# A 5120-row graph layer on one Trainium2 core: a third product summed in spare banks between rows of the second sweep

## The reference, cut to what matters

```
e   = blockwise (par * (diag * x) @ W + x)
h   = adj @ (adj.T @ e)
x1  = layernorm(x + layernorm(h) * gamma + beta + x)      # layer 0
T0  = x1
T1  = adj @ T0
T2  = 2 * adj @ T1 - T0
T3  = 2 * adj @ T2 - T1
out = layernorm(x1 + T0 @ w0 + T1 @ w1 + T2 @ w2 + T3 @ w3 + bias)   # layer 1
```

## Time and profile before

| what | value |
|---|---|
| median of 3 runs | 1223.32 us (1223.15 to 1223.8) |
| the profiled execution, its own time | 1222.88 us |
| its span in the profile | 1221.1 us |
| busy share of PE, DVE, ACT, POOL | 91%, 76%, 27%, 21% |
| moved over the span | 350.82 MB, mean 287 GB/s |
| second sweep | 866.0 to 1025.4 us |
| third sweep with its outputs | 1025.4 to 1206.7 us |

### The profile page before, as it was taken

The page is one execution under the profiler, slowest core; times in us unless marked ns, Lnnn a source line. Parts: engine busy times, 40 slices in busy tenths (PEclk is TensorE's granted clock), DMA queues, the critical chain, the costliest instruction groups (busy, mean ns, idle before and its releaser), DMA issues.

```text
span 1221.1 us, 13860 instructions
## 1 busy us (share of the span) xinstructions
PE 1109.2 (91%) x4995; PEld 480.7 (39%) x5004; DVE 928.5 (76%) x960; ACT 332.0 (27%) x594; POOL 257.0 (21%) x420
## 2 busy tenths in 40 slices
PE   4999999999999996899889999999899999598794
PEld 3444454444454442444333333444344443122221
DVE  2698798999998998698777766665666667588784
ACT  1456456466465562400100000000100000011010
POOL 0476555463453543100000000000000000011111
PEclk9999999999999998899999999999999999799898
DMA  7999999999999975899999999999999999999991
GB/s 225 301 291 299 278 299 305 297 295 282 300 274 288 282 206 121 181 291 309 238 347 347 337 313 308 306 293 255 262 331 333 325 305 328 348 311 342 352 353 33
DMA packets 372731, 350.82 MB, mean 287 GB/s; under 512 B 11613, under 2 KB 371333, under 8 KB 372693
## 3 DMA queue, kind: packets, MB, share of 16 engines
q1 hardware_dynamic: 259092, 237.35, 69.6%
q10 hardware_dynamic: 110880, 110.11, 31.6%
q0 software_dynamic: 2720, 2.86, 1.0%
HBM read 348.97 MB, written 1.31 MB: 287 GB/s over the span
## 4 chain that ended last, share of the span: by engine, by line
PE 54%; DVE 13%; SPq 12%; ACT 10%; ACTq 5%; issue 4%; DMA 1%; POOL 0%; DVEq 0%
PE bank L1176 30%; ACT terms L775 9%; SPq L337 7%; ACTq L279 5%; SPq L326 4%; DVE turned L496 4%; PE bank L1227 4%; PE bank L1189 3%; PE bank L1006 2%; PE bank L1046 2%; PE bank L1034 2%; PE bank L1018 2%; PE bank L1058 2%; DVE shared L516 2%; DVE xq L496 1%
## 5 line engine op out<-in xcount | busy, mean ns | idle before, releaser
L1176 PE MATMUL bank<-turned,terms 128*128 128x512 f32 x680 | 301.6, 596 | 4.8 <-DVE turned L496 3.3
L386 POOL COPY raw<-raw 32x512 f32<-32x512 f32 x320 | 194.2, 607 | 239.6 <-DVE raw L533 190.2
L516 DVE STREAM_TRANSPOSE shared<-shared 32x512 f32<-32x512 f32 x320 | 224.0, 700 | 4.1
L1006 PE MATMUL bank<-shared 128*64 128x256 f32 x1600 | 206.4, 385 | 6.9 <-DMA shared<-in_adj 6.9
L496 DVE STREAM_TRANSPOSE turned<-raw 128x2048 f32<-128x2048 f32 x72 | 165.1, 2301 | 58.3 <-PE bank L1176 49.5
L496 DVE STREAM_TRANSPOSE turned<-shared 128x2048 f32<-128x2048 f32 x68 | 156.1, 2303 | 60.6 <-PE bank L1176 46.4
L775 ACT COPY terms<-terms 32x512 f32<-32x512 f32 x320 | 197.0, 616 | 8.3 <-issue 3.2
L1176 PEld LDWEIGHTS bank<-turned,terms 128*128 128x128 f32 x680 | 126.6, 190 | 170.9 <-issue 163.3
L431 POOL DMA_DIRECT2D out<-scratch x40 | 21.7, 549 | 681.3 <-DVE scratch L725 681.2
L1006 PEld LDWEIGHTS bank<-shared 128*64 128x64 f32 x1600 | 112.0, 136 | 88.2 <-issue 32.6
L1069 PE MATMUL bank<-turned,t_quart 128*64 128x512 f32 x160 | 82.7, 603 | 8.5 <-DVE t_quart L540 8.5
(11 more groups left out here) (143 smaller groups left out, 1060.2 us busy)
## 6 DMA issues: line engine op xcount, KB each, us to landing
shared<-in_adj SPq DMA_DIRECT2D x100, 1024.0 KB, 10.8
raw<-in_adj SPq DMA_DIRECT2D x106, 512.0 KB, 10.6
raw<-in_adj ACTq DMA_DIRECT2D x106, 512.0 KB, 12.4
shared<-in_adj SPq DMA_DIRECT2D x104, 512.0 KB, 10.6
shared<-in_adj ACTq DMA_DIRECT2D x104, 512.0 KB, 12.6
raw<-in_adj SPq DMA_DIRECT2D x80, 256.0 KB, 7.6
xq<-in_x POOLq DMA_DIRECT2D x40, 32.0 KB, 6.2
out<-scratch POOLq DMA_DIRECT2D x40, 32.0 KB, 5.2
```

Of the source, the lines that this page charges most:

```text
L386: last = nc.gpsimd.tensor_copy(moved[Q32 * c:Q32 * (c + 1), :, :, Q32 * q:Q32 * (q + 1)], beside[Q32 * q:Q32 * (q + 1), :, c, :, :])
L516: last = nc.vector.transpose(low_turned[Q32 * c:Q32 * (c + 1), :, :, Q32 * q:Q32 * (q + 1)], low[Q32 * q:Q32 * (q + 1), :, :, Q32 * c:Q32 ...
L1006: last = nc.tensor.matmul(t_bank[H * odd:H * (odd + 1), 0:PW], e[:, s * SB + b, :], panels[slot][:, s * SB + b, :], start=(k == 0 and b < ...
L1176: last = nc.tensor.matmul(sum_bank[parity][:, :], terms[:, c * GB + i, columns], turned[place][:, i * BANK:(i + 1) * BANK], start=(first a ...
```

## The change

Five of the 55 units exist only because the second and third sweep visit the same pair of tiles apart: the pairs (g, g+1) and (g, g) of an even g. The change lets these pairs be loaded once (`held` gives a tile the unit that already holds its pair): the diagonal tiles of rows 8, 6, 4 and 2 (`DIAG`) are used one to five tiles after the row's last tile of the second sweep, for T3 alone, into the upper half of the row's own bank, and (0, 0) is used seven tiles after (0, 1). The slot stays taken until then. In the new order `late` there are still 100 tiles, numbered 0 to 99, in 50 units (50 to 99): 45 of kind UP (128 columns), 4 DIAG (64 columns, all into one half of the bank), 51 LOW (the tiles of the third sweep that are left). 24 LOW tiles, of rows 9, 8, 7 and 6, stand between the UP tiles, each row in a bank of its own (`LOW_BANK`), after the UP units named in `AFTER_UP`; the other 27 are tiles 73 to 99. Rows are completed after the tiles 76 (row 6), 78 (9), 79 (0), 83 (8), 87 (7), 89 (5), 91 (2), 93 (4), 95 (1) and 99 (3). Before, they were complete after tiles 54, 55, 64, 66, 74, 77, 84, 88, 94 and 99.

ACT no longer issues units only ahead of the copy of a row: at every tile n it first issues what comes free with tile n + 3 or earlier. The rows of T2 whose diagonal tile comes later are copied in two parts (`take_up`, `take_late_diag`). PE's `turn_p` of the first output waits for the copy of row 6, because both use bank 4. The output's banks become 5 and 0.

```diff
-        out_bank = banks[1:3]
+        out_bank = [banks[5], banks[0]]
...
+        ROWS3 = [6, 9, 0, 8, 7, 5, 2, 4, 1, 3]
+        LOW_BANK = {9: 0, 8: 1, 7: 2, 6: 4, 5: 7, 0: 6, 4: 6, 2: 1, 1: 2, 3: 6}
+        EARLY_LOW = [(9, 4), (9, 3), (8, 3), (7, 3), (9, 2), (8, 2), (7, 2), (6, 2), (9, 1), (8, 1), (7, 1), (6, 1)]
+        AFTER_UP = [2, 5, 7, 9, 10, 12, 14, 16, 17, 19, 21, 23]
+        LAST_LOW = [(5, 2), (6, 0), (9, 0), None, (5, 1), (8, 0), (4, 1), (7, 0), (5, 0), (2, 0), (4, 0), (1, 0),
+                    (3, 1), (3, 0)]
...
+        for g in ROWS2_ORDER:
+            for window in range(NG // SPAN - 1, (g + 1) // SPAN - 1, -1):
+                late += [(UP, g, c) for c in (SPAN * window + 1, SPAN * window) if c > g]
+                ups += 1
+                if open_diag is not None:
+                    late.append((DIAG, open_diag, open_diag))
+                    open_diag = None
+                if ups in AFTER_UP:
+                    late += low_pair(*EARLY_LOW[AFTER_UP.index(ups)])
+            if g % SPAN == 0 and g > 0:
+                open_diag = g
+        for pair in LAST_LOW:
+            late += low_pair(*pair) if pair else [(LOW, 0, 0)]
...
+            u = held.get(key) if n >= NG * NG else len(loads) - 1
+            if loads and u is not None and loads[u][0:2] == key and (n > NG * NG or u == len(loads) - 1):
+                loads[u] = (*key, n)
...
+            for n in range(len(late)):
                 late_tile(n)
...
+                if n - 1 - FINISH in low_end:
+                    finish(low_end.index(n - 1 - FINISH))
...
-            for i in range(NG):
-
-                done = [j for j in range(i) if END3[i - 1] <= END3[j] + 2 < END3[i]]
-                if i >= 1:
-                    load_through(START3 + END3[i - 1] + 1)
-                    take_p(i - 1)
-                    take_output(i - 1)
...
+            for n, (kind, g, c) in enumerate(late):
+
+                unwritten = [write_at[i] for i in range(NG - 1) if up_end[i] >= n]
+                unfinished = [low_end[j] + 1 + FINISH for j in range(NG) if low_end[j] + 3 >= n]
+                load_through(NG * NG + min([n + 3] + unwritten + unfinished))
+                if n - 1 in low_end:
+                    take_p(low_end.index(n - 1))
+                    take_output(low_end.index(n - 1))
+                if n == len(late) - 2:
+                    take_p(NG - 1)
+                if n in up_end:
+                    take_up(up_end.index(n), g)
+                if kind == DIAG:
+                    take_late_diag(n, g)
+                if n in low_end:
+                    take_low(low_end.index(n))
+                if n - 3 in low_end:
+                    j = low_end.index(n - 3)
+                    load_through(NG * NG + low_end[j] + 1 + FINISH)
                     root(2 * NS + j, GB)
...
+            def add_late_diag(t, place, g, parity, middle=None):
...
+                    last = nc.tensor.matmul(sum_bank[parity][H:P, :], terms[:, g * GB + i, 2 * H:3 * H],
+                                            turned[place][:, i * BANK:(i + 1) * BANK], start=False,
...
             def turn_p(i, g):
+                if i == 0:
+                    pe.wait_ge(row_copied, ROWS2 + 1)
```

More of the change, by code:

```diff
@@ new lines, in resnorm_chebyshev @@
+        for pair in LAST_LOW:
+            late += low_pair(*pair) if pair else [(LOW, 0, 0)]
+        late_tiles = [(g, c) for _, g, c in late]
+        up_end = [max(n for n, (kind, row, _) in enumerate(late) if kind == UP and row == g) for g in ROWS2_ORDER]
+        low_start = [min(n for n, (kind, row, _) in enumerate(late) if kind == LOW and row == g) for g in ROWS3]
+        low_end = [max(n for n, (kind, row, _) in enumerate(late) if kind == LOW and row == g) for g in ROWS3]
+        assert low_end == sorted(low_end) and len(late) == NG * NG
@@ L239, in resnorm_chebyshev @@
+        DIAGS = [g for kind, g, _ in late if kind == DIAG]
+        needed = [min(n for n, (kind, row, c) in enumerate(late) if c == g and n > up_end[i])
+                  for i, g in enumerate(ROWS2_ORDER)]
+        write_at = [min(up_end[i] + 4, needed[i]) for i in range(NG - 1)]
         first_rows = [(g, DOWN[k + i]) for k in range(0, NG, 2) for g in range(2) for i in range(2)]
         T2 = T1 + NG * NG
-        late_tiles = sweep2 + sweep3
         row_end = {n: T1 + ((n + 1) * NG if n else PAIR - 2) for n in range(NG)}
@@ L262, in resnorm_chebyshev @@
         load_of = []
+        held = {}
         for n, (g, c) in enumerate(all_tiles):
[L264 to L268 removed]
+            key = (g, c // SPAN)
+            u = held.get(key) if n >= NG * NG else len(loads) - 1
+            if loads and u is not None and loads[u][0:2] == key and (n > NG * NG or u == len(loads) - 1):
+                loads[u] = (*key, n)
+            else:
+                loads.append((*key, n))
+                u = len(loads) - 1
+            if n >= NG * NG:
+                held[key] = u
+            load_of.append(u)
+        assert all(load_of[n] < SLOTS or loads[load_of[n] - SLOTS][2] < n for n in range(len(all_tiles)))
         def free_after(u):
@@ L1180, in add_tile, with add_tile_halves @@
                 last.then_inc(tile_used, 1)
-            def add_tile_halves(t, place, c, parity, first, last_tile, middle=None):
+            def add_tile_halves(t, place, c, bank, first, last_tile, middle=None):
                 pe.wait_ge(tile_turned, t + 1 + RAW)
@@ new lines, in between @@
+            def between(n):
+                if n - 1 in up_end:
+                    i = up_end.index(n - 1)
+                    turn_row(ROWS1 + i, i % 2, H)
+                if n - 1 in low_end:
+                    turn_p(low_end.index(n - 1), ROWS3[low_end.index(n - 1)])
+                if n == len(late) - 2:
+                    turn_p(NG - 1, ROWS3[-1])
+                if n == len(late) - 1:
+                    output_sums(NG - 1, ROWS3[-1])
+                    output_p(NG - 1, ROWS3[-1])
@@ new lines, in _ @@
+            for n, (kind, g, c) in enumerate(late):
+                t, place = T2 + n, late_place(n)[0]
+                middle = lambda: between(n)
+                if kind == UP:
+                    i = ROWS2_ORDER.index(g)
+                    if i == 0:
+                        pe.wait_ge(u_written, NG)
+                    elif c == NG - 1 and g + 2 in DIAGS:
+                        pe.wait_ge(late_diag_kept, DIAGS.index(g + 2) + 1)
+                    if i > 0 and c == g + 1:
+                        pe.wait_ge(row_written, ROWS1 + i)
+                    add_tile(t, place, c, i % 2, c == NG - 1, c == g + 1, slice(H, 3 * H), middle)
+                elif kind == DIAG:
+                    i = ROWS2_ORDER.index(g)
+                    pe.wait_ge(row_written, ROWS1 + i + 1)
+                    add_late_diag(t, place, g, i % 2, middle)
+                else:
+                    j = ROWS3.index(g)
+                    if c < NG - 1:
+                        pe.wait_ge(row_written, ROWS1 + ROWS2_ORDER.index(c) + 1)
+                    add_tile_halves(t, place, c, banks[LOW_BANK[g]], n == low_start[j], n == low_end[j], middle)
+                if n - 2 in low_end:
+                    turn_output(low_end.index(n - 2))
+                if n - 1 in low_end:
+                    j = low_end.index(n - 1)
+                    output_sums(j, ROWS3[j])
+                    output_row(j)
+                    output_p(j, ROWS3[j])
```

122 lines of the change are left out of this document (47 added, 75 removed).

## The result

The changed kernel takes 1254.32 us (median of 4 runs, 1253.32 to 1255.78) where the kernel before takes 1223.56 beside it: 2.4% slower, ratio 1.0244, 95% interval 1.023 to 1.0258. The forecast was 1237 with a range from 1214 to 1262, so the direction and the range held, and the loss is 31 us where I had 14. The profiled execution took 1253.32 us, its span is 1251.4.

What follows compares the result with a forecast made beforehand. PE was taken to bound the second sweep, transfers at 6.03 us a unit the third. Steps put PE's end at 1220.2; + 14.4 to the span's end, + 1.8 execution, + 0.4 median gave 1237 us, range 1214 to 1262.

Steps and rivals of the forecast that it cites:

- Step 2: From unit 54's landing to the turn of tile 79: transfers, not PE, set this stretch; tile 79 turned at 1112.9.
- The terms 35 x 6.03, 12 and 6.6: Up to tile 79's turn: 35 units at 6.03 us, 12 us for three held-slot stops, 6.6 us for three last turns.
- rival C: ScalarE's copies of the last four T2 rows come late, up to 23 us, taken as 20: 1257 us; chance 0.21.
- the 25 us of cover: Up to tile 79: 25 us between PE and the transfers, said to hide most late copies of T2 rows.
- Step 3: Row 6's copy stands behind eight blocked ScalarE issues after tile 79's turn: 14.7 us, to 1127.6; bounds 3.4 to 24.
- Rival A: At row 6's copy the queue has room for all eight transfers: 3.4 instead of 14.7 us, total 1226; chance 0.14.
- the rule that I weighed: Several issuing engines only save small issue time; earlier issues bring nothing, the eight-issue block costs 3.4 us: sum 1226.
- Step 4: From row 6's copy to PE's end: 0.6 + 1.4 + 37.6 + 40, 2.0 for the last row, 11 us waits: 1220.2.
- near half behind it: Sign of a right forecast: PE's granted clock near half after its 15 to 20 us idle before `turn_p`.
- The end behind PE: From PE's end to the end of the span: 14.4 us, which no edit touches.
- Rival B: Transfers set the end, faster, with outputs beside the last ten units: 1202 us; chance 0.15.
- The 30 us of transfers are saved, and given back: Five spared units save 30 us, lost to stops before tile 79 and to outputs at the end with little cover.

Runs made afterwards that it cites:

- e15: Changed kernel, ScalarE issuing behind the copies and for n + 1 instead of n + 3, eight early pairs instead of twelve, all 55 units loaded: 1228.35 us.
- e11: Changed kernel, ScalarE issuing behind the copies and for n + 1 instead of n + 3, eight early pairs instead of twelve, (0, 0) loaded again (51 units): 1215.96 us.
- e9: Changed kernel with both cures: ScalarE issues behind the copies of the tile's step, and for n + 1 instead of n + 3; 50 units: 1229.6 us.
- e13: Changed kernel, ScalarE issuing for n + 1 instead of n + 3 only up to the last tile of the second sweep: 1252.55 us.
- e12: Changed kernel with all four quarters of the late units issued by SyncE, none by ScalarE: 1373.71 us.
- e8: Changed kernel with one number changed: ScalarE issues what tiles through n + 1 set free, not n + 3, still ahead of the copies: 1231.43 us.
- e14: Changed kernel, ScalarE issuing for n + 1 instead of n + 3 only behind the second sweep: 1239.71 us.
- e3: Changed kernel with its new order but no slot held, so 55 units are loaded: 1251.02 us.
- e16: Changed kernel, ScalarE issuing behind the copies and for n + 1 instead of n + 3, twelve early pairs, (0, 0) loaded again (51 units): 1219.89 us.
- e5: Changed kernel with ScalarE's two quarters of each unit in the second and third sweep issued by GpSimd instead: 1334.22 us.

## Why the forecast was right in direction and short in size

**What bounds the kernel.** No run tests on the kernel before that the transfers set its third sweep; the nearest is that with ScalarE mostly free and a balanced order, four units more cost 12.4 us (e15 against e11), half of their 24. In the changed kernel neither PE nor transfers bound the end; ScalarE's program order did.

**Step 2, tile 79 turned at 1112.9.** Measured 1116.42 + 2.27 = 1118.7, 5.8 later. e9 has this stretch without ScalarE's late copies, and at most units DVE waits there for the transfer; where it does, the start of its turn is the landing (in brackets its idle time and that it was the DMA):

```profile
885.66 2.31 DVE L539 STREAM_TRANSPOSE turned<-shared 128x2048 f32<-128x2048 f32 x1 [0.48 <-DMA shared<-in_adj]
891.71 2.31 DVE L539 STREAM_TRANSPOSE turned<-raw 128x2048 f32<-128x2048 f32 x1 [3.74 <-DMA raw<-in_adj]
...
941.68 2.31 DVE L539 STREAM_TRANSPOSE turned<-raw 128x2048 f32<-128x2048 f32 x1 [1.75 <-DMA raw<-in_adj]
...
957.92 2.31 DVE L539 STREAM_TRANSPOSE shared<-shared 128x2048 f32<-128x2048 f32 x1 [4.82 <-DMA shared<-in_adj]
...
1109.63 2.31 DVE L539 STREAM_TRANSPOSE turned<-shared 128x2048 f32<-128x2048 f32 x1 [1.06 <-DMA shared<-in_adj]
...
1114.06 2.27 DVE L539 STREAM_TRANSPOSE xq<-shared 128x2048 f32<-128x2048 f32 x1
```

A unit is 6.05 us behind the last (891.71 - 885.66), and a stop shows as two units in 16.24 (957.92 - 941.68), 4.1 over; with the smaller gaps near it the stops sum to 1109.63 - 885.66 - 35 x 6.05 = 12.2 us. The terms 35 x 6.03, 12 and 6.6 (from 1109.63 to the end of the turn that begins at 1114.06: 6.7) were right, the 12 in part by luck: stops of 4.1 us stand at two of the three units that wait for a held slot (65 and 76), none at the third (58), and gaps of 1.2 to 1.4 us at three other places make up the sum. Unit 54 landed at 885.7, not 883.2. The changed kernel is another 2.4 later at tile 79, and all of it arises ahead of its own row:

```profile
960.53 2.31 DVE L539 STREAM_TRANSPOSE shared<-shared 128x2048 f32<-128x2048 f32 x1 [4.04 <-DMA shared<-in_adj]
```

This is 2.6 behind e9's 957.92. Ahead of it DVE stood behind PE, which had waited for the first late copy of a T2 row:

```profile
884.07 0.68 PE L1265 MATMUL bank<-ident,scratch 64*128 64x64 f32 x4 [5.18 <-ACT scratch L934]
```

That is rival C, which was partly there: PE waited 16.9 us in all for these copies. Of the four places that C names, two came (4.7 us in tile 34, 6.8 in tile 60), and the 25 us of cover took them in, since the distance to e9 is 2.6 us ahead of them and 2.4 behind; the wait that reached tile 79, by 2.4 us, is that of row 7 in tile 3, which C doesn't name. e13, which takes these waits away, is 1.8 us faster.

**Step 3, eight issues, 14.7 us.** Right: 14.4 measured, in the place and form forecast (0.92 for two, 7.53 for four, 5.87 for two), and PE idle 16.3 us. Rival A is refuted by this, and so is, for this kernel, the rule that I weighed, from the Trainium skill, "DMA: Bandwidth & Descriptors", section "Issuing engines are not separate DMA queues". By it several issuing engines save only a time that is small beside the transfer. The measurements differ: eight issues blocked ScalarE for 14.4 us, and with one issuing queue for two (e12) the changed kernel took 1373.71 us, 9.5% more.

**Step 4, the term that failed.** "I take twice that for nine rows, 11 us." From the copy of row 6 to PE's end it took 1237.1 - 1133.2 = 103.9 us where the sum has 92.6. So the tail waits with all that they bring cost 22.3 us, not 11, and that is 11.3 of the 16.8 us by which the span was missed; step 2 gives 5.8 and step 3 takes back 0.3.

The 11.3 are not longer waits. Here is that stretch as a window, then the window and the PE records behind the wait for row 0's turned input, and the same kind of tile where nothing was waited for:

```profile
1133.20:1237.10 103.90, 92.20 (x338) 27.61 (x338) 63.62 (x82) 19.57 (x39) 19.52 (x36) 0.89 0.60 172
1156.30:1161.80 5.50, 5.50 (x11) 1.05 (x11) 2.87 (x5) 0.78 (x2) 1.77 (x4) 0.50 1.09 319
```
```profile
1158.18 3.68 PE L1245 MATMUL bank<-turned,terms 128*64 128x512 f32 x8
...
1201.85 1.94 PE L1245 MATMUL bank<-xq,terms 128*64 128x512 f32 x8
```

PE is idle for 11.7 us of the 103.9 (103.9 - 92.2), where the sum has 13.6 for its idle time (0.6 + 2.0 + 11). It is busy for 92.2, where the sum has 1.4 + 37.6 + 40 = 79.0. The granted clock is 0.50, the level of 1.2 GHz, behind the wait of 16.3 us (1133.8 to 1138.0), behind that of 3.0 (1156.3 to 1161.8) and the first of 3.3 (1174.1 to 1179.6), and 0.73 on the mean behind the second (1191.6 to 1195.4). A tile behind the 3.0 takes 3.6 us (1158.18 to 1161.79), where it takes 1.9 at 2.4 GHz. Against the same records at 1.00 (1208.60 to 1212.05 here, 1113.10 to 1116.38 in e9) this comes to about 10 us: 2.4 behind the first wait, then 3.0, 2.7 and 1.6. The sum prices every tile and output of step 4 at full clock; the clock stands among its signs ("near half behind it") and at nothing in its terms. The other 3 us are outputs that cost more than 4.0 (two tiles and an output 7.75, not 7.4). That the waits themselves, 9.6 us, came near their 11 is luck: they are three of 3.0 to 3.3 us, not nine of 1.2.

The waits' cause I had in the text (ScalarE takes a row only after it issued what the tile three further on sets free), and I priced it by the waits of the kernel before, where ScalarE doesn't do that. It is a ring: the issue waits for the turn of tile n + 3, the turn stands on DVE behind a norm that waits for PE's `turn_output` (`DVE scratch L763 <- PE bank L1397`, 20.6 us), PE waits in `output_p` for the copy that stands behind the issue. It closes at rows 8 and 7, completed four tiles after the one before, 6.6 to 7.0 us too long each time, 2.7 to 3.0 of it PE's lower clock inside the ring. e8 and e14, which open it by two tiles, take back 22.9 and 14.6 us, and in e9 a row of this kind takes 11.2 (1158.51 to 1169.69):

```profile
1158.51 1.07 PE L1389 MATMUL bank<-shared,w_p 64*64 64x512 f32 x2
1169.69 1.07 PE L1389 MATMUL bank<-shared,w_p 64*64 64x512 f32 x2
```

The end behind PE, 14.4 forecast, is 1251.4 - 1237.1 = 14.3.

**Rival B** didn't come: the changed kernel's spared units weren't worth anything (e3). "The 30 us of transfers are saved, and given back" was right, but not for the reason alone that I gave, the outputs without cover. With both cures and (0, 0) loaded again, the same twelve pairs give 1219.89 us (e16), so most of what was given back was ScalarE's order, and it was not needed.

## What to carry to other kernels

An engine that both issues transfers and does work that others wait for should do that work first, and issue only what is free now: a look ahead by a few tiles makes it stand in the waits of other engines, and its own work with it. Price such a wait by the rule of the new program (which turn does the issue need, and when is it there), not by the waits that the old one shows; and price what PE does behind a wait by the clock that it gets there. Before sparing a transfer by keeping a buffer longer, look at what comes free in one burst at its release: here four such holds paid while PE had other work, and the fifth, at the seam, cost 9.7 us with eight issues in a row at its release.

## What the runs showed of the hardware

- The choice of issuing queues changes the rate of these transfers (512 KB, each into 32 partitions): both queues 347 GB/s, SyncE's alone 212, SyncE's with GpSimd's 231 and 239. No run has transfers of another shape, so whether a queue or its 32 partitions set the 212 is open. In e5 GpSimd issues a transfer in 0.65 us and isn't held, and the DMA share is 1.02 at 231 GB/s; the share of the profile is thus no measure of bytes.

```profile
1018.68 1.30 POOL L323 DMA_DIRECT2D raw<-in_adj  x2 [6.08 <-DVE xq L551]
```

- PE's clock after a wait: in the changed kernel the four records of L1367 at 1133.80 take 1.06 us, and 0.63 in the next such place; the granted clock is 0.50 from 1133.8 to 1138.0, and 0.50 for 5.5 us behind a wait of only 3.0 us (1156.3 to 1161.8). Its mean over 1066 to 1166 is 0.85, in e16 0.95. A wait thus costs more than its length: about 10 us in this kernel's tail, beside 16.3 and 11.1 us of idle time.
